# Routed expert blocks: up weights stationary, token rows moving, and no transposes of the hidden values

## The reference

```
x = x + 0.5 * ffn(layernorm(x))
x = x + attn(layernorm(x))
x = x + 0.5 * ffn(layernorm(x))

ffn:  shared = (silu(x @ sw1.T) * (x @ sw2.T)) @ sw3.T          # hidden 2048
      top 2 of 8 experts for each row, by a router
      h12 = x @ w12[e].T; h = silu(h12[:256]) * h12[256:]      # hidden 256
      routed = sum over the 2 experts of score * (h @ w3[e].T)
      ffn = shared + routed
```

## Time and profile before

| | |
|---|---|
| three runs | 1470.33, 1473.96, 1477.14 us |
| median | 1473.96 us |
| profiled execution: span, first to last instruction | 1469.7 us (nothing is recorded around it) |
| PE busy | 1419.1 us, 97% of the span |
| PE weight loads busy | 679.7 us |
| DVE, ACT, POOL busy | 944.8, 552.4, 501.0 us |
| mean granted clock of PE | 0.998 of full speed |

### The profile page before, as it was taken

The page is one execution under the profiler, slowest core; times in us unless marked ns, Lnnn a source line. Parts: engine busy times, 40 slices in busy tenths (PEclk is TensorE's granted clock), DMA queues, the critical chain, the costliest instruction groups (busy, mean ns, idle before and its releaser), DMA issues.

```text
span 1469.7 us, 22015 instructions
## 1 busy us (share of the span) xinstructions
PE 1419.1 (97%) x7642; PEld 679.7 (46%) x7642; DVE 944.8 (64%) x1295; ACT 552.4 (38%) x1153; POOL 501.0 (34%) x424
## 2 busy tenths in 40 slices
PE   4999999999999999899999999999999999999998
PEld 2444444444444544445454444444444444444443
DVE  5778853333348989898889889979925733333243
ACT  4566323333233433345435454345233213333211
POOL 2321132221244475252625434444322122221353
PEclk9999999999999999999999999999999999999999
DMA  8999659887493467075526552445338168888594
GB/s 305 305 350 320 267 146 209 200 182 192 172 277 125 156 196 220 30 244 135 153 72 186 150 166 73 121 160 140 112 101 257 59 188 213 192 190 185 187 321 165
DMA packets 233724, 272.63 MB, mean 186 GB/s; under 512 B 132242, under 2 KB 156818, under 8 KB 230162
## 3 DMA queue, kind: packets, MB, share of 16 engines
q1 hardware_dynamic: 198594, 166.34, 39.7%
q10 hardware_dynamic: 23664, 67.66, 14.5%
q0 software_dynamic: 11360, 37.23, 9.4%
HBM read 168.39 MB, written 72.88 MB: 164 GB/s over the span
## 4 chain that ended last, share of the span: by engine, by line
PE 63%; DVE 10%; issue 8%; DMA 4%; POOL 2%; ACT 2%; SPq 1%; POOLq 0%; ACTq 0%; DVEq 0%
PE bank L1484 25%; PE bank L1607 13%; PE bank L1498 12%; PE bank L1632 7%; DVE region L1147 3%; DMA rows<-sorted_y,slots 1%; PE side L1120 1%; PE side L1620 1%; DVE region L1153 1%; POOL rows L665 1%; DMA x2d<-rows 1%; DVE sgh L1854 1%; PE side L1253 1%; DMA region<-region 1%; POOL hs L1812 1%
## 5 line engine op out<-in xcount | busy, mean ns | idle before, releaser
L1484 PE MATMUL bank<-xT,wb 128*128 128x512 bf16 x2688 | 615.5, 381 | 22.6 <-DMA xT<-region 17.6
L1484 PEld LDWEIGHTS bank<-xT,wb 128*128 128x128 bf16 x2688 | 257.7, 98 | 323.9 <-issue 29.2
L1812 POOL TENSOR_TENSOR hs<-sgh,hs 128x512 bf16<-128x512 f32 x126 | 161.9, 1285 | 629.1 <-ACT hs L1704 628.2
L1498 PE MATMUL bank<-wb,hs 128*128 128x512 bf16 x1536 | 358.0, 380 | 0.2 <-POOL hs L1812 0.2
L1498 PEld LDWEIGHTS bank<-wb,hs 128*128 128x128 bf16 x1536 | 147.8, 98 | 173.9 <-issue 2.9
L1607 PE MATMUL bank<-wr,region 128*128 x912 | 221.7, 379 | 0.0
L1704 ACT ACTIVATE hs<-sgh 128x512 bf16<-128x512 f32 x128 | 81.3, 635 | 340.2 <-DVE sgh L1854 337.4
L1854 DVE TENSOR_TENSOR sgh<-bank,sgh 128x512 f32<-128x512 f32 x128 | 87.9, 687 | 155.8 <-PE bank L1484 154.6
L1147 DVE TENSOR_TENSOR region<-region 128x1024 f32<-128x1024 f32 x128 | 183.0, 1454 | 0.9
L1801 POOL DMA_INDIRECT region<-xnd,idxs x78 | 74.6, 957 | 221.8 <-DMA region<-region 213.5
L1153 DVE TENSOR_REDUCE region<-region 128x256 f32<-128x2048 f32 x64 | 146.3, 2286 | 2.2
(11 more groups left out here) (182 smaller groups left out, 1351.6 us busy)
## 6 DMA issues: line engine op xcount, KB each, us to landing
wb<-wsplit ACTq DMA_DIRECT2D x42, 1024.0 KB
wb<-wsplit ACTq DMA_DIRECT2D x42, 512.0 KB, 4.4
sorted_y<-region SPq DMA_DIRECT2D x78, 256.0 KB
wsplit<-wb SPq DMA_DIRECT2D x8, 1536.0 KB, 7.4
wr<-wall SPq DMA_DIRECT2D x6, 1536.0 KB, 9.7
rows<-x SPq DMA_DIRECT2D x32, 256.0 KB, 4.9
region<-xln SPq DMA_DIRECT2D x128, 64.0 KB, 3.7
xnd<-rows SPq DMA_DIRECT2D x30, 256.0 KB, 4.0
```

What stands on the lines that cost most here:

```text
L1484: m = e.matmul(ps[:], wb[:, w % 2, wp, at:at + P], xt[:, xp, c, :], start=(i == 0), stop=(i == 3 * NDC - 1))
L1498: m = e.matmul(psD[tt][:], hs[:, s % 2, hp, tt * P:(tt + 1) * P], wb[:, w % 2, wp, at:at + D], start=(first and i == 0), stop=(last and i ...
L1812: e.tensor_tensor(hs[:, s % 2, 1, :], sgh[:, s % 2, :], hs[:, s % 2, 0, :], ALU.subtract).then_inc(S("h_lo").sem, 1)
```

## The change

The operands of the up product swap places. Before, the block's 128 rows stood in the array and 512 weight columns moved. Now 128 by 128 pieces of the expert's weights stand there and the block's 128 rows move. The 512 outputs are four quarters `q`, each an accumulation of 12 matmuls into 128 columns of the same PSUM bank, so a block's up product is 48 matmuls of 128 columns. Its output has the hidden index on the partitions. So `hidden_T` (four transposes on PE) and DVE's copy of them are gone; ACT and DVE write the high and low parts straight into `hT`. `down_of` is renamed `down` and is otherwise the same, now waiting on `r_hTl`. For the last block, the wait on `r_mul` that stood in `hidden_T`'s chain now stands before the next slot's second product.

```diff
-        psH, psHT, psY = [banks[1], banks[0]], psS[1].bitcast(BF16)[:, 0:2 * HC], banks[4:6]
+        psH, psY = [banks[1], banks[0]], banks[4:6]
...
-                    def words_of(k, wp, at):
+                    def words_of(k, wp, at, n):
 
-                        return wr[:, bass.ds(expert[k], 1), wp, at:at + D].rearrange("p o w -> p (o w)")
+                        return wr[:, bass.ds(expert[k], 1), wp, at:at + n].rearrange("p o w -> p (o w)")
...
-                        n = 0
-                        for c in range(NDC):
-                            if c == NDC // 2:
-                                between()
-                            for wp, xp in PASSES:
-                                m = e.matmul(psH_of(k)[:], xsT[k % RX][:, xp * D + c * P:xp * D + (c + 1) * P],
-                                             words_of(k, wp, c * D), start=(n == 0),
-                                             stop=(n == 3 * NDC - 1))
-                                n += 1
+                        for q in range(2 * KT):
+                            n = 0
+                            for c in range(NDC):
+                                for wp, xp in PASSES:
+                                    m = e.matmul(psH_of(k)[:, q * P:(q + 1) * P], words_of(k, wp, c * D + q * P, P),
+                                                 xsT[k % RX][:, xp * D + c * P:xp * D + (c + 1) * P], start=(n == 0),
+                                                 stop=(n == 3 * NDC - 1), skip_group_check=True)
+                                    n += 1
                         m.then_inc(S("r_h").sem, 1)
 
-                    def hidden_T(k):
-                        e.wait_ge(S("r_hbl").sem, NB * f + k + 1)
-                        if k >= 1:
-                            e.wait_ge(S("r_hT").sem, NB * f + k)
-                        for a in range(2):
-                            for kt in range(KT):
-                                n = a * KT + kt
-                                m = e.transpose(psHT[:, n * P:(n + 1) * P], hb[k % 2][:, a, kt * P:(kt + 1) * P],
-                                                identb[:])
-                        m.then_inc(S("r_HT").sem, 1)
...
                     for k in range(1, NB):
-                        up(k, lambda: hidden_T(k - 1))
+                        up(k)
                         if k == 1:
                             e.wait_ge(S("ev").sem, 4 * (8 if f else 1) + 4)
-                        down_of(k - 1)
+                        down(k - 1)
...
-                        e.activation(hb[k % 2][:, 0, :], hf[k % 2], ACT.Copy).then_inc(S("r_hbh").sem, 1)
+                        e.activation(hT[k % 2][:, 0].rearrange("p k n -> p (k n)"), hf[k % 2], ACT.Copy).then_inc(
+                            S("r_hTh").sem, 1)
...
-                        e.tensor_tensor(hb[k % 2][:, 1, :], hf[k % 2], hb[k % 2][:, 0, :],
-                                        ALU.subtract).then_inc(S("r_hbl").sem, 1)
-
-                    def hidden_T(k):
-                        e.wait_ge(S("r_HT").sem, NB * f + k + 1)
-                        if k >= 2:
-                            e.wait_ge(S("r_y").sem, NB * f + k - 1)
-                        e.tensor_copy(hT[k % 2].rearrange("p a k n -> p (a k n)"), psHT).then_inc(S("r_hT").sem, 1)
+                        high, low = (hT[k % 2][:, a].rearrange("p k n -> p (k n)") for a in range(2))
+                        e.tensor_tensor(low, hf[k % 2], high, ALU.subtract).then_inc(S("r_hTl").sem, 1)
```

More of the change, by code:

```diff
@@ L1336, in macaron @@
         hf = [take(HC) for _ in range(2)]
-        hb = [take(HC, BF16).rearrange("p (a n) -> p a n", a=2) for _ in range(2)]
         hT = [take(HC, BF16).rearrange("p (a k n) -> p a k n", a=2, k=KT) for _ in range(2)]
@@ L1480, in products @@
                             if gu and s in ROUTED_AT:
-                                block[ROUTED_AT.index(s)][1](NB - 1)
+                                down_of[ROUTED_AT.index(s)](NB - 1)
                         for wp, xp in PASSES:
@@ L1560, in slot @@
                     products(psG, s, 0, "h_g", 0)
-                    if s in ROUTED_AT:
-                        block[ROUTED_AT.index(s)][0](NB - 1)
                     sides(s, 1)
@@ L1567, in slot @@
                         e.wait_ge(S("h_mul").sem, s)
+                    if s in ROUTED_AT:
+                        e.wait_ge(S("r_mul").sem, NB * (ROUTED_AT.index(s) + 1))
                     products(psU, s, 1, "h_u", 2)
@@ L1584, in flush, with up @@
                         down(s, tt)
-                block = {}
+                down_of = {}
                 def routed(f):
-                    def words_of(k, wp, at):
-                        return wr[:, bass.ds(expert[k], 1), wp, at:at + D].rearrange("p o w -> p (o w)")
+                    def words_of(k, wp, at, n):
+                        return wr[:, bass.ds(expert[k], 1), wp, at:at + n].rearrange("p o w -> p (o w)")
                     def expert_of(k):
                         expert[k] = e.value_load(bexp[0:1, f, k:k + 1], min_val=0, max_val=E - 1)
-                    def up(k, between):
+                    def up(k):
                         if k:
@@ L1601, in up, with down @@
                             e.wait_ge(S("r_mul").sem, NB * f + k - 1)
-                        n = 0
-                        for c in range(NDC):
-                            if c == NDC // 2:
-                                between()
-                            for wp, xp in PASSES:
-                                m = e.matmul(psH_of(k)[:], xsT[k % RX][:, xp * D + c * P:xp * D + (c + 1) * P],
-                                             words_of(k, wp, c * D), start=(n == 0),
-                                             stop=(n == 3 * NDC - 1))
-                                n += 1
-                        m.then_inc(S("r_h").sem, 1)
-                    def hidden_T(k):
-                        e.wait_ge(S("r_hbl").sem, NB * f + k + 1)
-                        if k >= 1:
-                            e.wait_ge(S("r_hT").sem, NB * f + k)
-                        for a in range(2):
-                            for kt in range(KT):
-                                n = a * KT + kt
-                                m = e.transpose(psHT[:, n * P:(n + 1) * P], hb[k % 2][:, a, kt * P:(kt + 1) * P],
-                                                identb[:])
-                        m.then_inc(S("r_HT").sem, 1)
-                    def down_of(k):
-                        e.wait_ge(S("r_hT").sem, NB * f + k + 1)
+                        for q in range(2 * KT):
[6 more added lines that the diff above has]
+                                    n += 1
+                        m.then_inc(S("r_h").sem, 1)
+                    def down(k):
+                        e.wait_ge(S("r_hTl").sem, NB * f + k + 1)
                         if k >= 2:
@@ L1631, in down_of @@
                                 at = W3OFF + kt * D
-                                m = e.matmul(psY[k % 2][:], hT[k % 2][:, hp, kt, :], words_of(k, wp, at),
+                                m = e.matmul(psY[k % 2][:], hT[k % 2][:, hp, kt, :], words_of(k, wp, at, D),
                                              start=(n == 0), stop=(n == 3 * KT - 1))
@@ L1640, in routed @@
                     e.wait_ge(S("side_read").sem, pieces_before(ROUTED_AT[f]))
-                    up(0, lambda: None)
+                    up(0)
                     flush(ROUTED_AT[f] - 1)
@@ L1644, in routed @@
                     for k in range(1, NB):
-                        up(k, lambda: hidden_T(k - 1))
+                        up(k)
                         if k == 1:
                             e.wait_ge(S("ev").sem, 4 * (8 if f else 1) + 4)
-                        down_of(k - 1)
-                    block[f] = hidden_T, down_of
+                        down(k - 1)
+                    down_of[f] = down
                 for s in range(START, SLOTS_ALL):
@@ L1744, in hidden @@
                         if k >= 2:
-                            e.wait_ge(S("r_HT").sem, NB * f + k - 1)
-                        e.activation(hb[k % 2][:, 0, :], hf[k % 2], ACT.Copy).then_inc(S("r_hbh").sem, 1)
+                            e.wait_ge(S("r_y").sem, NB * f + k - 1)
+                        e.activation(hT[k % 2][:, 0].rearrange("p k n -> p (k n)"), hf[k % 2], ACT.Copy).then_inc(
+                            S("r_hTh").sem, 1)
                     def result(k):
@@ L1949, in hidden @@
                         if k >= 2:
-                            e.wait_ge(S("r_hbl").sem, NB * f + k - 1)
+                            e.wait_ge(S("r_hTl").sem, NB * f + k - 1)
                         e.tensor_tensor(hf[k % 2], psH_of(k)[:, HC:2 * HC], sg[k % 2], ALU.mult).then_inc(
                             S("r_mul").sem, 1)
-                        e.wait_ge(S("r_hbh").sem, NB * f + k + 1)
-                        e.tensor_tensor(hb[k % 2][:, 1, :], hf[k % 2], hb[k % 2][:, 0, :],
```

(11 more changed lines are left out.)

## The result

The changed kernel takes 1586.6 us (median of 4 runs, 1584.1 to 1592.3) against 1472.2 for the kernel before in the runs beside it: 1.077 times as long, 95% interval 1.074 to 1.080. It is 114 us slower; the prediction said 90 (1564 us).

The account below looks back on a forecast made before the run. The prediction took PE's array to bound the kernel before and PE's sequencer the changed one's routed stages: +45.1 us each, 1469.7 + 90.2 = 1559.9 us profiled, 1564 timed. Range 1495 to 1625, leaving out 2 in 10.

Parts of the forecast that it names:

- Array: PE's array in a routed block: up product 2.65 us against 2.59, transposes -0.22, block 3.94 against 4.10.
- Sequencer: PE's sequencer in a routed block: 36 register instructions at 0.124 us plus waits, 5.32 us, so the array waits.
- theory S: From the follow-up runs: PE's sequencer sets the block's time, by its register instructions.
- A stage: One routed stage: first up product 3.97, flush 0.5, 38 blocks of 5.32; 206.6 us against 161.3.
- DVE and ACT: In the routed stages: DVE loses a 0.42 us copy a block, worth nothing; the 1.8 us silu-to-subtraction chain stays covered.
- A: Routed blocks: register instructions run ahead, the array stays the bound, block 3.94 us, total 1462 us; chance 0.12.
- B: Register instructions in routed blocks cost 0.095 to 0.115 us each, blocks 4.27 to 4.99, total 1487 to 1543; chance 0.08.
- C: Up product's weight loads from a register address not hidden: block 6.0 us, 1622, or 8.6, 1825; chance 0.09 together.
- D: PE's clock drops because its array idles in short gaps: block 7.9 us, +296, total 1770 us; chance 0.05.
- What I said the profile would show: PE in the routed stages: 206 us span, "issue" idle time, register instructions 0.124 apart, up products 3.97 us, clock 1.00.

Follow-up runs that it names:

- the kernel before with constant addresses: Kernel before, with the up product's weights at a build-time address (expert k modulo 8), leaving 4 register instructions a block: 1476.1 us, ratio 1.0009.
- the constant addresses: Changed kernel, with the up product's weights at a build-time address (expert k modulo 8), its 32 register instructions a block gone: 1463.9 us, ratio 0.994.
- the experiment in quarters: Kernel before, rows in the array and transposes kept, up product in four column quarters (48 matmuls of 128 columns, 32 register instructions): 1595.9 us, ratio 1.084.

## Why the prediction was right, and where it was short

*Array.* 2.65 us was forecast for the up product; 2.68 was measured once nothing held it back. The gain of the transposes and the block of 3.94 were right to 0.03 us.

*Sequencer.* This was the deciding term and the right one. The distance of 0.124, read from five distances in the kernel before, is the distance in the changed kernel. The mechanism is shown from both sides: with fewer register instructions, or without the sequencer's bounds check, the time falls; with fewer matmuls it does not.

*The size.* The step that was short is the block's sum "36 x 0.124 = 4.46, the expert's number with the first wait 0.75, the down product's wait 0.1: 5.32 us" (the terms make 5.31). It measured 5.62. The missing 0.30 us a block, 76 blocks in the two stages, make 23 of the 24 us by which the forecast was low. They are the long distances: one in about eight register instructions is 0.07 longer on average. Four to five of them a block are the 0.3 us. The window from which I took 0.124 holds only five distances, too few for one of a period of 8, and it ends just before a long one. A window of line 1607 from 216.49 to 216.73 us in the kernel before has the sixth register instruction and the seventh:

```profile
L1607 PEldq FUSED_REGOPS  x2: 46/46/46, 216.5 to 216.7; - x2
```

They are 0.215 apart in the trace. The earlier trace rows already had the two distances from 216.5 to the last one at 216.8, together 0.3 and not 0.25. The four instructions of a down product in the earlier trace rows hide one too: the last of their three distances is 0.145. In the rest of the kernel before, the sequencer ran ahead and then waited, so a long distance there could be taken for a full queue. What tells the two apart is the regular place of the long ones (last section). The expectations of the experiments used the measured 0.3, and theory S, in the form that the run left standing where it had two, came within 4.1 us of the measured time in all nine kernels. The largest miss is the 1472 for the kernel before with constant addresses (1476.1); the kernel before itself took 1475.5 beside it.

*A stage.* In the first stage up(0) and flush were as forecast in kind: from up(0)'s start to flush's is 220.40 - 216.28 = 4.12 us, against 3.97, and the sequencer got ahead during flush. In the second stage up(0) took 1269.23 - 1266.44 = 2.79. There the sequencer had begun with it at 1263.4, three us before the array was free, which no term of the prediction had. It saved little: the stage is under 0.3 us shorter than the first.

*DVE and ACT.* DVE's busy time fell by 33 us (944.8 to 911.8) and that bought nothing, as said: with constant addresses the array ran its 3.97 us a block without a gap.

*Rivals.* A (the array stays the bound) is what the constant addresses show: a gain of 9 us, had the addresses been free; the forecast gave it 12. B (cheaper register instructions) and C (weight loads not hidden) didn't happen. D didn't: the mean granted clock is 0.998 in both kernels, although in the first stage 4 in 10 of the up product's matmuls start more than 0.07 us after the one before. Its price was read from the start of the run, where the rows print a clock of 1.00 and only the matmuls' distances show the slower pace: 0.427 us for most of the first ten, 0.216 afterwards. The 0.081 us of the Trainium skill (TensorE: Matmul & The Clock Gate, Back-to-back issue gap) for a pair at 128 columns isn't borne out: 48 in a row take 0.056 each.

*What I said the profile would show.* That PE would be idle, with "issue" as the reason, was wrong: its matmuls' records cover the gaps. The two up products in the lines of the chain take 4.4 and 4.2 us from their first matmul's start to the down product's, where 3.97 was forecast, since the register instructions are 0.124 apart but for the long distances. The down product's matmuls are 0.215 to 0.225 apart throughout both stages, as said. The chain's 1.47 for six of them is five such distances and the whole record of the last, 0.38; the next up product starts 1.30 us after the down product. Whether an execution without any records would have the same distances isn't shown by a run here.

No version that beats both kernels came out of this. The faster experiments read wrong weights. Fewer distinct addresses a block with the right weights, or array work with constant addresses between the blocks while the sequencer forms them, might give the 9 us; neither was tried.

## What to carry to other kernels

Count distinct run-time addresses as well as matmuls. On PE each costs the sequencer one instruction, here 0.124 us and 0.13 with the long ones, beside matmuls of 512 columns as of 128. A 512-column matmul (0.215) hides one. A 128-column matmul (0.056) doesn't, and the three that share two addresses here (0.17 against 0.26) don't either. Before cutting an operand into smaller pieces, add up the sequencer's time for the block from the distances between its records and set it against the array's. PE's busy share will not show which of the two is ahead: look at how far apart the starts are.

## What was not expected of the hardware

While the sequencer is never held up, one distance in 8 register instructions is longer: mostly 0.14 to 0.30 us in place of 0.124. It comes after 8 register instructions whether 32 or 24 instructions lie between, and with a DMA share of 0.58 or of 0.13.

A rival that no experiment was made for is that it comes once in a fixed time, since 8 distances are always about 1 us. The trace of the changed kernel rules it out. The 251 times with 8 register instructions between have 1.0 to 1.3 us from one to the next. 42 times there are 6, with the load of the expert's number and the check's register instruction between: 8 again, but 1.5 us or more. Counted over the register instructions, the check's included, and the loads of the expert's number, 324 of the 340 long distances stand at one place in eight, the same throughout a stage.

The long distances did not come with the change either. In the kernel before, 70 of the 73 distances between 0.14 and 0.4 stand at one place in eight, if the wait in the middle of the up product (line 1616) is counted too; the experiment in quarters needs the same for its own such wait, with 297 of 312. The waits at the start of the up product and before the down product do not count, and why isn't known. What the long distance is stays open; the runs say that it goes with the number of such instructions and adds 6 to 7% to the sequencer's time for them.
